# A graph network on one core: relation tables made bare inside the edge MLP's loop, their gate and bias applied in the relation pass

## The chip, the cores and the metric

The kernel runs on one core of a Trainium2 chip. The metric is the device time of one execution in microseconds (us). Before the change the median of three runs is 4499.05 us (4494.59 to 4503.68).

## The reference

Four graph layers work on 6250 nodes of 128 features and 106250 edges (50000 random pairs in both directions and a loop for every node, sorted by destination). After each, the result is added to the nodes and layer-normalised.

```python
x = _layernorm(x + gat_0(x, src, dst))
x = _layernorm(x + edge_mlp(x, src, dst, edge_attr_32))
x = _layernorm(x + relations(x, src, dst, edge_type_8))
x = _layernorm(x + gat_1(x, src, dst))

# edge_mlp, per edge, then per node
h   = gelu(_layernorm(concat(x[src], edge_attr) @ W1 + b1))
agg = segment_sum(h @ W2 + b2, dst)
out = gelu(_layernorm(concat(x, agg) @ Wu + bu)) + x

# relations: 8 relation types, one matrix, bias and gate each
msg  = (h @ W[rel])[src] + bias_term[rel]
gate = sigmoid(sum(msg * gate_weight[rel]) + gate_bias[rel])
out  = relu(segment_sum(msg * gate, dst) + h @ loop_weight)
```

The gate's argument is linear in the node's row, so it can be had from one product of the node with a matrix of 128 x 8 folded from W and the gate weights, plus a folded bias.

## The kernel before

The nodes are 49 tiles of 128, kept in SBUF. The edges are 104 groups (NG) of 1024, each group 8 tiles of 128 edges. A pass over the edges works through the groups in order: GpSimd (POOL) fetches the source rows of a group from a table in device memory with eight indirect DMAs (831 in a pass, since the last group is not full) into a ring of 8 groups (RING); a matrix of zeros and ones, made by VectorE (DVE) from the destinations, turns the sum over destinations into matmuls on TensorE (PE); DVE adds each group's sums (`p_sum`, PSUM) into the node accumulator `acc`. There are four such passes: attention (L723, gathers at L840), the edge MLP (`mlp_pass` L1464, gathers at L1593), relations (`rel_pass` L1192, gathers at L1254) and attention again.

The work on nodes is cut into 13 units of four tiles (the last two have three and two). Each engine's program is written out in order: step by step, an engine does its stage for group `step - lag`, and then the pieces of the units whose start `unit.at` plus the piece's lag is that step (`drive` L609, `weave` L619, where the order within a step is written). A unit starts when the groups that hold its edges have been summed, and at least six groups (APART) after the unit before; the last two start at steps 100 and 106. Engines meet at semaphores alone, and each stands still at a wait until it is met.

In a step of the MLP loop PE multiplies edge attributes (L1872), DVE adds them to the gathered rows (L1624), ScalarE (ACT) squares (L1789) and takes a root (L1791), DVE scales (L1630, L1632), ACT applies the gelu (L1799), and PE sums (L1889), into two alternating banks. DVE adds the sums (L1646) three steps after the gather. A unit's pieces follow: the node product, an inner normalisation, its gelu, the residual (L1722), the outer normalisation.

The relation tables, 49 tiles of 128 nodes x 8 relations x 128 features, are made after all sums of the MLP loop have been added (`sums_done`): PE turns the node tiles (L1938), ACT copies them out (L1843), PE makes the gate products (L1946) and the products with the relation matrices (L1954), both in PSUM banks that the loop used. DVE adds the gate bias (L1739), ACT takes the sigmoid (L1849), DVE adds the relation's bias to a whole tile while taking it out of PSUM (L1746) and multiplies half of it by the gate (L1750), ACT the other half (L1855), and SP stores the tile with one 512 KB transfer (L1574). The relation pass's first gather waits for all stores. In that pass a row of the table is a finished message of 512 bytes: it is gathered, and summed with the one-hot matrix (L1281, L1411, L1287).

Of the kernel before, what the change touches and what calls it, by code (L numbers as in the profile page):

```python
# [23 lines left out]
P = 128  # L24
# [9 lines left out]
RING = 8  # L34
HALF = 4
# [7 lines left out]
NORMED_AT = 14  # L43
ONE, AS = F, F + 1
TAB = AS + 2 * H
SUMS = AS + H
EPS = 1e-5
# [6 lines left out]
Unit = namedtuple("Unit", "u first tiles after at tab")  # L54
OfTable = namedtuple("OfTable", "lag")
# [12 lines left out]
def units_of(n, e, nt, ng):  # L68
# [8 lines left out]
    for u, m in enumerate(sizes):  # L77
        end = (first + m) * P
        after = ng - 1 if end >= n else min(ng - 1, -(-(end + SLACK) * e // (n * GE)) - 1)
        at = max(after, at + APART)  # L80
        units.append(Unit(u, first, m, after, at, 0))
        first += m
    start, end = ng + 2, at + NORMED_AT + 1
    spread = [start + (end - start) * unit.u // max(1, len(units) - 1) for unit in units]
    return tuple(unit._replace(tab=max(at, unit.at + NORMED_AT + 1)) for unit, at in zip(units, spread))

# [46 lines left out]
class Net:  # L133


    def __init__(self, nc, ctx, sh, ins, out):
# [23 lines left out]
        self.rel_b = sb("rel_b", [P, R, F])  # L160
# [14 lines left out]
        self.rel_table = dram("rel_table", (sh.NP * R, F))  # L175
# [414 lines left out]
def begins(unit, lag):  # L590

    return unit.tab + lag.lag if isinstance(lag, OfTable) else unit.at + lag
# [84 lines left out]
def landed(sh, n):  # L677


    return 16 * sum(len(given(sh, k)) for k in range(n % RING, n + 1, RING))  # L680

# [510 lines left out]
def rel_pass(net):  # L1192
# [3 lines left out]
    names = ["always", "weights_in", "onehot", "summed", "added", "index_in", "pool_passed", "sp_passed", "dve_passed", "act_passed", "pe_passed",  # L1196
             "x_turned", "xt_ready", "node_product", "variance", "rooted", "factors", "normed", "new_turned", "new_ready", "tab_product",
             "tab_done", "kept", "stored0", "stored1", "bound", "bound_all"]
    with phase(net, names, ["gathered"], RING) as s:
# [3 lines left out]
        rows = s.sb("rows", [P, RING, T, F])  # L1203
        hot = s.sb("hot", [P, HALF, T, P])
        lw = s.sb("lw", [P, F])
# [20 lines left out]
        def _(sp):  # L1226
            def load_slow(g):
                sp.dma_start(idx[:, :], net.rel_index[:, bass.ds(g, 1), :].rearrange("p g t -> p (g t)")).then_inc(s.index_in, 16)
                sp.dma_start(dsts[:, :], a["dst_cols"][bass.ds(g, 1), :, :].rearrange("g p t -> p (g t)")).then_inc(s.index_in, 16)
                sp.wait_ge(s.added, (g + 1) * sh.NT)  # L1230
                sp.sem_inc(s.sp_passed, 1)
# [5 lines left out]
            sp.dma_start(lw[:, :], a["L2_gnn_loop_weight"]).then_inc(s.weights_in, 16)  # L1237

# [11 lines left out]
        def _(pool):  # L1250
# [8 lines left out]
            def gather_slow(g):  # L1259
                pool.wait_ge(s.index_in, (g + 1) * 32)  # L1260
# [17 lines left out]
        def _(dve):  # L1278
# [3 lines left out]

            def add(n):
                first = window(dve, net, n)
                dve.wait_ge(s.summed, n + 1)
                part = net.acc[:, 0, bass.ds(first, P)]
                nc.vector.tensor_tensor(part, part, p_sum[n % 2][:, 0:P], ALU.add)  # L1287
                dve.drain().then_inc(s.added, 1)

            def residual(unit):  # L1290
# [4 lines left out]
                nc.vector.memset(net.acc[:, 0, columns(unit)], 0.0)  # L1295
# [24 lines left out]
            def slow_group(g):  # L1320
                dve.wait_ge(s.index_in, (g + 1) * 32)
                dve.wait_ge(s.gathered[0], (g + 1) * 16 * T)
                dve.sem_inc(s.dve_passed, 1)

            def slow_window(v, k):
# [6 lines left out]
                part = net.acc[:, 0, bass.ds(k * P, P)]  # L1332
                nc.vector.tensor_tensor(part, part, p_sum[0][:, 0:P], ALU.add)
                dve.drain().then_inc(s.added, 1)

            nc.vector.tensor_copy(p_iota[:, :], net.iota_row[:, :])
            dve.drain().then_inc(s.always, 1)
# [30 lines left out]
        def _(act):  # L1368
            def copy_x(unit):
# [27 lines left out]
            def fast():  # L1397
                drive(sh, [], pieces)

            def slow():  # L1400
                drive_units(sh, pieces)
# [3 lines left out]
        def _(pe):  # L1405
            def add_up(n):
                pe.wait_ge(s.onehot, n + 1)
                pe.wait_ge(s.gathered[n % RING], landed(sh, n))
                wait(pe, s.added, n - 1)
                for t in range(T):  # L1410
                    end = nc.tensor.matmul(p_sum[n % 2][:, 0:P], rows[:, n % RING, t, :], hot[:, n % HALF, t, :], start=(t == 0), stop=(t == T - 1))  # L1411
                end.then_inc(s.summed, 1)
# [7 lines left out]
            def multiply(unit, fast):  # L1420
# [23 lines left out]
            def slow_window(v, k):  # L1444
                pe.wait_ge(s.onehot, v + 1)
                for t in range(T):
                    end = nc.tensor.matmul(p_sum[0][:, 0:P], rows[:, 0, t, :], hot[:, 0, t, :], start=(t == 0), stop=(t == T - 1))
                end.then_inc(s.summed, 1)
# [4 lines left out]
            def fast():  # L1453
                drive(sh, [(add_up, 0)], pieces(True))
# [5 lines left out]
            pe.wait_ge(s.weights_in, 16)  # L1460
# [3 lines left out]
def mlp_pass(net):  # L1464
# [4 lines left out]
             "x_turned", "xt_ready", "node_product", "variance", "rooted", "factors", "inner_normed", "node_scaled", "activated", "normed", "tab_turned", "tab_copied", "gate_product", "gate_logits", "gate_ready", "tab_product", "tab_read", "dve_scaled", "act_scaled",  # L1469
             "index_in", "pool_passed", "sp_passed", "dve_passed", "act_passed", "pe_passed"]  # L1470
    with phase(net, names, ["gathered"], RING, ["operands_in", "hot_in"], HALF, ["stored"], TABS) as s:
# [3 lines left out]
        rows = s.sb("rows", [P, RING, T, HID])  # L1475
# [581 lines left out]
```

## Time and profile before

| what | time |
|---|---|
| median of three runs | 4499.05 us |
| the profiled execution, its span | 5314.6 us |
| PE busy | 3112.7 us (59%) |
| DVE busy | 2515.0 us (47%) |
| ACT busy | 1308.4 us (25%) |
| POOL busy | 3165.2 us (60%) |

The profile is one execution of the program, and its span, the only time that it gives for itself, is 18% above the median. Busy times are of compute instructions and of POOL's gathers; the shares are averages over stages that differ. A row of a timeline gives start, duration, engine, line, what is written from what, and in brackets how long the engine had been idle and what released it ("issue" where it waited for nothing the profile shows, "remote" for a queue that it doesn't know).

### The profile page before, as it was taken

The numbers are of one execution on the slowest core, as the hardware profiler recorded it, in microseconds if no ns is written. First come the engines' busy times: TensorE is split into PE (matmuls) and PEld (weight loads), VectorE is DVE, ScalarE is ACT, GpSimd is POOL, SyncE is SP. The second block draws the span as 40 slices with busy tenths as digits, with TensorE's granted clock in tenths as the row PEclk, the third lists the DMA queues.
The fourth block names the chain that finished last, engine by engine and source line by source line (L and its number), as shares of the span: only waits on it lengthen the run. The fifth ranks groups of instructions, "written<-read, shape, count | busy, mean of one in ns | idle before, by whom it ended". The sixth has DMA issues, their size and how long they took to land. (4 is left out here: it accounts for less than half of the span.)

```text
span 5314.6 us, 52198 instructions
## 1 busy us (share of the span) xinstructions
PE 3112.7 (59%) x15416; PEld 2793.1 (53%) x15416; DVE 2515.0 (47%) x5316; ACT 1308.4 (25%) x3470; POOL 3165.2 (60%) x3335
## 2 busy tenths in 40 slices
PE   2666666666377787777871323333332666666666
PEld 2665666566366676666731223323231666666665
DVE  2344444445377878777870111112121454554555
ACT  0010010011267777777760000000000011111111
POOL 5666666663566666666206666666654666666662
PEclk6556556666689888988895566665665565555656
DMA  5444444443444444444241111111112333333331
GB/s 140 128 144 139 151 142 140 151 140 110 138 134 145 147 144 144 143 144 148 81 189 47 48 49 49 50 49 47 52 43 67 97 95 97 99 95 97 98 96 52
DMA packets 284107, 567.22 MB, mean 107 GB/s; under 512 B 108648, under 2 KB 157034, under 8 KB 283802
## 3 DMA queue, kind: packets, MB, share of 16 engines
q0 software_dynamic: 119664, 280.17, 20.3%
q1 hardware_dynamic: 157082, 278.92, 15.4%
q10 hardware_dynamic: 7056, 4.56, 0.3%
q8 instruction: 131, 2.15, 0.2%
q14 instruction: 174, 1.43, 0.1%
HBM read 465.83 MB, written 97.56 MB: 106 GB/s over the span
## 5 line engine op out<-in xcount | busy, mean ns | idle before, releaser
L840 POOL DMA_INDIRECT rows<-gat_table,src_i x1662 | 1568.6, 944 | 861.4 <-issue 464.9
L1593 POOL DMA_INDIRECT rows<-mlp_table,src_i x831 | 789.5, 950 | 527.0 <-issue 303.8
L1254 POOL DMA_INDIRECT rows<-rel_table,rel_i x831 | 783.9, 943 | 494.8 <-issue 343.4
L1129 PE MATMUL p_sum<-rows,hot 128*128 128x133 f32 x3328 | 781.6, 425 | 14.2 <-DVE rows L906 12.5
L1121 PEld LDWEIGHTS p_adc<-adw,hot_t 128*128 128x128 f32 x3328 | 688.1, 314 | 178.0 <-DVE hot_t L880 127.5
L1121 PE MATMUL p_adc<-adw,hot_t 128*128 128x8 f32 x3328 | 678.0, 342 | 147.7 <-DVE hot_t L880 108.4
L1129 PEld LDWEIGHTS p_sum<-rows,hot 128*128 128x128 f32 x3328 | 735.9, 326 | 17.2 <-DVE rows L906 15.6
L1411 PE MATMUL p_sum<-hot,rows 128*128 128x128 f32 x1664 | 324.5, 363 | 715.9 <-DVE hot L1281 365.9
L1411 PEld LDWEIGHTS p_sum<-hot,rows 128*128 128x128 f32 x1664 | 298.6, 272 | 744.3 <-DVE hot L1281 381.2
L1061 ACT COPY sums<-p_sum 128x133 f32<-128x133 f32 x208 | 56.4, 271 | 2211.6 <-DMA rel_index<-rel_i 1902.6
L1889 PE MATMUL p_sum<-hot,rows 128*128 128x128 f32 x3328 | 476.0, 310 | 201.8 <-ACT rows L1799 107.7
L1889 PEld LDWEIGHTS p_sum<-hot,rows 128*128 128x128 f32 x3328 | 461.3, 224 | 236.5 <-ACT rows L1799 123.5
L1136 PE MATMUL p_turn<-ident,sums 128*128 128x128 f32 x208 | 90.7, 436 | 781.1 <-ACT sums L1061 724.7
L906 DVE TENSOR_TENSOR rows<-rows,p_weight 128x1024 f32<-128x1024 f32 x208 | 253.7, 1220 | 610.5 <-ACT p_weight L1056 448.2
L1872 PE MATMUL p_pre<-w1e,eat 128*128 128x256 f32 x1664 | 436.8, 415 | 105.3 <-issue 104.4
L1136 PEld LDWEIGHTS p_turn<-ident,sums 128*128 128x128 f32 x208 | 35.5, 171 | 834.5 <-ACT sums L1061 772.8
L1287 DVE TENSOR_TENSOR acc_t<-acc_t,p_sum 128x128 f32 x104 | 29.8, 286 | 864.3 <-remote 775.9
L1872 PEld LDWEIGHTS p_pre<-w1e,eat 128*128 128x128 f32 x1664 | 337.3, 209 | 172.5 <-issue 123.3
L1789 ACT ACTIVATE junk<-rows 128x256 f32<-128x256 f32 x832 | 335.6, 404 | 294.5 <-DVE rows L1624 179.0
L1624 DVE TENSOR_TENSOR rows<-rows,p_pre 128x1024 f32<-128x1024 f32 x208 | 247.6, 1218 | 281.1 <-PE p_pre L1872 112.2
L1630 DVE SCALAR_TENSOR_TENSOR rows<-rows,stats,p_affine 128x256 f32<-128x256 f32 x832 | 335.1, 475 | 8.3
L886 DVE TENSOR_TENSOR z<-rows,p_adc 128x32 f32<-128x32 f32 x208 | 39.0, 188 | 561.1 <-remote 312.0
(239 smaller groups left out, 3693.9 us busy)
## 6 DMA issues: line engine op xcount, KB each, us to landing
drow<-in_dst_rows SPq DMA_DIRECT2D x208, 512.0 KB
hot_table<-hot SPq DMA_DIRECT2D x104, 512.0 KB
hot<-hot_table SPq DMA_DIRECT2D x104, 512.0 KB
rows<-gat_table,src_i POOLq DMA_INDIRECT x1662
rel_table<-rows SPq DMA_DIRECT2D x49, 512.0 KB, 2.6
eat<-in_edge_t SPq DMA_DIRECT2D x104, 128.0 KB
rows<-mlp_table,src_i POOLq DMA_INDIRECT x831
rows<-rel_table,rel_i POOLq DMA_INDIRECT x831
```

The source lines that it names most:

```text
L840: pool.indirect_dma_start(out=rows[:, n % RING, t, :], out_offset=None, in_=net.gat_table[:, :], in_offset=bass.IndirectOffsetOnAxis(ap=ne ...
L906: nc.vector.tensor_tensor(hr, hr, wt, ALU.mult).then_inc(s.messages, 1)
L1121: end = nc.tensor.matmul(p_adc[k][:, t, 0:2 * H], hot_t[:, k, t * P:(t + 1) * P], adw[:, half, :], start=True, stop=True)
L1129: end = nc.tensor.matmul(p_sum[:, 0:SUMS], hot[:, n % HALF, t, :], rows[:, n % RING, t, 0:SUMS], start=(t == 0), stop=(t == T - 1))
L1254: pool.indirect_dma_start(out=rows[:, n % RING, t, :], out_offset=None, in_=net.rel_table[:, :], in_offset=bass.IndirectOffsetOnAxis(ap=ne ...
L1411: end = nc.tensor.matmul(p_sum[n % 2][:, 0:P], rows[:, n % RING, t, :], hot[:, n % HALF, t, :], start=(t == 0), stop=(t == T - 1))
L1593: pool.indirect_dma_start(out=rows[:, n % RING, t, :], out_offset=None, in_=net.mlp_table[:, :], in_offset=bass.IndirectOffsetOnAxis(ap=ne ...
L1624: nc.vector.tensor_tensor(rows[:, slot, tt, :], rows[:, slot, tt, :], p_pre[half][:, :, :], ALU.add).then_inc(s.pre, 1)
L1630: nc.vector.scalar_tensor_tensor(rows[:, slot, t, :], rows[:, slot, t, :], stats[:, slot, 1, t:t + 1], p_affine[:, 0, :], ALU.mult, ALU.mult)
L1789: nc.scalar.activation(junk[:, t % (T // 2), :], rows[:, slot, t, :], ACT.Square, accum_out=stats[:, slot, 0, t:t + 1])
L1872: end = nc.tensor.matmul(p_pre[half][:, j, :], eat[:, ring, half, :], w1e[:, j, :], start=True, stop=True)
L1889: end = nc.tensor.matmul(p_sum[k][:, b, :], rows[:, n % RING, t, b * F:(b + 1) * F], hot[:, half, t, :], start=(t == 0), stop=(t == T - 1))
```

## The change

The relation table holds the bare product of node and relation matrix, and in a column of its own the gate's argument: rows of 129 values (REL) in place of 128. It is made inside the MLP loop, unit by unit, as soon as the unit's nodes are normalised: a turn at lag 15, the gate product at lag 16, and from lag 16 on a tile per step in two halves of four relations. PE makes a half in one PSUM bank `pt`, which holds the gate product too, in the columns of its first use; ACT alone copies it to one of four slots of `stage`, with the gate's arguments beside it; SP stores it (98 stores of 264 KB instead of 49 of 512 KB). To make room, the loop's sums have one bank instead of two (PE's sums of a group wait for DVE's add of the group before), the ring is 7 groups deep, and the relations' bias, 128 x 1024 in SBUF before, is no longer kept. DVE's order in a step begins with the add.

In the relation pass ACT takes the sigmoid of the gathered column (128 x 8 a group), DVE makes a matrix of edge by relation type, multiplies it and the gathered rows by the gate, and PE sums both with the one-hot matrix: the rows as before and, in eight matmuls more, the gates by type. DVE adds these to `acc` too, and the bias enters at the unit's product, as one more matmul of the summed gates with the 8 x 128 bias matrix. PE's sums come one step later than before, DVE's add two.

```diff
+MLP_RING = 7
+TURN_AT = NORMED_AT + 1
+GATE_AT = TURN_AT + 1
+REL = F + 1
 # relation pass
+            def kinds(half, given):
+                nc.vector.tensor_tensor(kind[:, half, :, :], tiled(given, T, R), over_tiles(net.iota_row[:, 0:R], T, R), ALU.is_equal)
+                dve.drain()
+            def weighted(slot, half, k):
+                nc.vector.tensor_tensor(kind[:, half, :, :], kind[:, half, :, :], tiled(gate[:, k, :], T, R), ALU.mult)
+                nc.vector.tensor_tensor(rows[:, slot, :, 0:F], rows[:, slot, :, 0:F], tiled(gate[:, k, :], T, F), ALU.mult)
+                return dve.drain()
+            def weigh(n):
+                kinds(n % HALF, types[:, n, :])
+                dve.wait_ge(s.gated, n + 1)
+                weighted(n % RING, n % HALF, n % 2).then_inc(s.weighed, 1)
...
+                nc.vector.tensor_tensor(gates, gates, p_sum[n % 2][0:R, P:2 * P], ALU.add)
...
-                drive(sh, [(one_hot, 0), (add, 1)], pieces)
+                drive(sh, [(one_hot, 0), (weigh, 1), (add, 2)], pieces)
...
+            def gates(n):
+                act.wait_ge(s.gathered[n % RING], landed(sh, n))
+                wait(act, s.weighed, n - 1)
+                nc.scalar.activation(gate[:, n % 2, :], rows[:, n % RING, :, F], ACT.Sigmoid).then_inc(s.gated, 1)
...
+                for t in range(T):
+                    nc.tensor.matmul(p_sum[k][0:R, P:2 * P], kind[:, half, t, :], hot[:, half, t, :], start=(t == 0), stop=(t == T - 1))
...
+                    nc.tensor.matmul(pu[:, t, :], net.acc[0:R, 1, cols], rb[:, :], start=False, stop=False)
 # MLP pass
-                    nc.vector.tensor_tensor(tab, p_tab[t % 2], net.rel_b[:, :, :], ALU.add).then_inc(s.tab_read, 1)
...
-                    nc.vector.tensor_tensor(tab[:, 0:by_dve, :], tab[:, 0:by_dve, :], tiled(gate[:, k, i, 0:by_dve], by_dve, F), ALU.mult).then_inc(s.dve_scaled, 1)
...
+            def copy_new(unit):
+                dve.wait_ge(s.new_turned, unit.u + 1)
+                nc.vector.tensor_copy(turned[:, 0:unit.tiles, :], pt[:, 0:unit.tiles, :]).then_inc(s.new_copied, 1)
...
+            def keep(unit, i, q):
+                h = part_of(unit, i, q)
                 act.wait_ge(s.gate_logits, unit.u + 1)
+                act.wait_ge(s.tab_product, h + 1)
+                wait(act, s.stored[h % TABS], 16 * (h // TABS))
+                nc.scalar.copy(staged(h)[:, :, F], logit[:, i, q * R // 2:(q + 1) * R // 2])
+                nc.scalar.copy(staged(h)[:, :, 0:F], pt[:, :, :]).then_inc(s.second_kept if q else s.first_kept, 1)
...
+            def fill(unit, i, q):
+                if q:
+                    pe.wait_ge(s.first_kept, unit.first + i + 1)
+                elif i:
+                    pe.wait_ge(s.second_kept, unit.first + i)
+                else:
+                    pe.wait_ge(s.gate_logits, unit.u + 1)
+                four = slice(q * R // 2, (q + 1) * R // 2)
+                nc.tensor.matmul(pt[:, :, :].rearrange("p r f -> p (r f)"), turned[:, i, :], net.rel_w[:, four, :].rearrange("p r f -> p (r f)"),
+                                 start=True, stop=True).then_inc(s.tab_product, 1)
...
-                wait(pe, s.added, n - 1)
+                wait(pe, s.added, n)
...
-                drive(sh, [(pre, 0), (add, 3), (scale, 1)], pieces(True))
+                weave(sh, [(add, 3, False), (pre, 0, False)] + [(fn, lag, True) for fn, lag in tables] + [(scale, 1, False)] + [(fn, lag, True) for fn, lag in weights + steps])
...
-                drive(sh, [(edges, 0), (add_up, 2)], pieces(True))
+                weave(sh, [(edges, 0, False)] + [(fn, lag, True) for fn, lag in turns + seconds] + [(add_up, 2, False)]
+                      + [(fn, lag, True) for fn, lag in pieces(True) + firsts])
```

## Rows read from the trace of the kernel before

**Rows 1.** Windows: the stages; busy us (x count), granted clock, DMA share, GB/s.
```profile
0.00:1430.00 1430.00, 859.75 (x4013) 792.66 (x4014) 623.58 (x1431) 129.90 (x460) 856.39 (x903) 0.61 0.47 138
1430.00:2600.00 1170.00, 908.78 (x5135) 801.41 (x5134) 910.73 (x1648) 850.22 (x2100) 729.02 (x767) 0.88 0.45 142
...
2900.00:4000.00 1100.00, 369.34 (x1958) 340.05 (x1959) 197.88 (x423) 43.67 (x95) 703.55 (x746) 0.61 0.19 48
4000.00:5315.00 1315.00, 805.08 (x3654) 751.71 (x3652) 631.38 (x1553) 158.91 (x490) 785.01 (x832) 0.59 0.33 90
...
```

**Rows 2.** Gather lines: ns min/median/max, first and last start; idle by releaser.
```profile
L840 POOL DMA_INDIRECT rows<-gat_table,src_i x1662: 938/944/1100, 51.1 to 5229.4; - x185
...
L1593 POOL DMA_INDIRECT rows<-mlp_table,src_i x831: 940/946/1324, 1339.3 to 2575.0; - x167
...
L1254 POOL DMA_INDIRECT rows<-rel_table,rel_i x831: 938/944/956, 2790.2 to 3967.9; - x167
...
  issue: 343.4, 799
...
```

**Rows 3.** Timeline of POOL in the MLP loop: start, us, instruction [idle before].
```profile
1530.83 0.95 POOL L1593 DMA_INDIRECT rows<-mlp_table,src_i  x1 [0.30 <-issue]
1532.09 0.95 POOL L1593 DMA_INDIRECT rows<-mlp_table,src_i  x1 [0.31 <-issue]
1535.14 0.95 POOL L1593 DMA_INDIRECT rows<-mlp_table,src_i  x1 [2.10 <-remote]
...
```

**Rows 4.** Windows summed over eleven stretches of the loop, and its scale line.
```profile
sum 1080.00, PE 838.67 PEld 738.56 DVE 837.88 ACT 788.04 POOL 690.27; mean PE 76.24 PEld 67.14 DVE 76.17 ACT 71.64 POOL 62.75
...
L1632 DVE TENSOR_TENSOR rows<-rows,p_affine x104: 2286/2287/2289, 1419.2 to 2637.4; 128x2048 f32<-128x2048 f32 x104
...
```

**Rows 5.** Timeline, DVE then POOL: the stretch between the two passes.
```profile
2645.63 0.42 DVE L1646 TENSOR_TENSOR acc_t<-acc_t,p_sum 128x256 f32 x1 [0.90 <-PE p_sum L1889]
...
2653.26 1.22 DVE L1746 TENSOR_TENSOR rows<-p_pre,rel_b 128x1024 f32<-128x1024 f32 x1
...
2790.21 0.95 POOL L1254 DMA_INDIRECT rows<-rel_table,rel_i  x1 [100.11 <-issue]
...
```

**Rows 6.** Lines of that stretch: busy us, mean ns, idle before.
```profile
L1954 PE MATMUL p_pre<-rel_w,hot 128*128 128x512 f32 x196 | 98.1, 647 | 8.8 <-DVE rows L1746 8.8
...
L1746 DVE TENSOR_TENSOR rows<-p_pre,rel_b 128x1024 f32<-128x1024 f32 x49 | 59.7, 1219 | 10.4 <-PE p_pre L1954 10.4
...
L1750 DVE TENSOR_TENSOR rows<-rows,gate 128x512 f32<-128x512 f32 x49 | 33.9, 692 | 8.9 <-ACT gate L1849 4.7
...
L1946 PE MATMUL p_affine<-rel_gate,hot 128*128 128x8 f32 x98 | 12.6, 254 | 3.3 <-ACT hot L1843 3.3
L1938 PE MATMUL p_sum<-ident,x_nodes 128*128 128x128 f32 x49 | 8.0, 284 | 7.4 <-ACT hot L1843 7.4
...
L1843 ACT COPY hot<-p_sum 128x512 f32<-128x512 f32 x11 | 6.2, 567 | 6.0 <-PE p_sum L1938 5.1 <-issue 0.9
...
```

**Rows 7.** Timeline of DVE: a node update's moments.
```profile
2646.61 0.86 DVE L1699 SCALAR_TENSOR_TENSOR o<-w2u,degree,pu 128x128 f32<-128x128 f32 x3 [0.56 <-PE pu L1929]
...
2648.95 0.18 DVE L705 RECIPROCAL work<-work 128x3 f32<-128x3 f32 x1
...
```

**Rows 8.** The table store, L1574: issue to landing.
```profile
DMA to landing us min/median/max: 2.6/2.6/3.8
```

**Rows 9.** The page's costliest groups: the relation pass's sums.
```profile
L1411 PE MATMUL p_sum<-hot,rows 128*128 128x128 f32 x1664 | 324.5, 363 | 715.9 <-DVE hot L1281 365.9
...
```

**Rows 10.** Timeline, all engines, near the MLP loop's last gathers.
```profile
2561.95 2.29 DVE L1632 TENSOR_TENSOR rows<-rows,p_affine 128x2048 f32<-128x2048 f32 x1
2563.09 0.95 POOL L1593 DMA_INDIRECT rows<-mlp_table,src_i  x1 [0.30 <-issue]
2564.16 0.68 DVE L1722 SCALAR_TENSOR_TENSOR x_nodes<-x_nodes,o 128x512 f32<-128x512 f32 x1
...
2564.34 1.32 POOL L1593 DMA_INDIRECT rows<-mlp_table,src_i  x1 [0.30 <-issue]
...
```

More of the change, by code:

```diff
@@ L53 @@
 Shapes = namedtuple("Shapes", "N E NT NP NW NG NB NBATCH BN units")
-Unit = namedtuple("Unit", "u first tiles after at tab")
-OfTable = namedtuple("OfTable", "lag")
+Unit = namedtuple("Unit", "u first tiles after at")
 def shapes_of(n, e):
@@ L80, in units_of @@
         at = max(after, at + APART)
-        units.append(Unit(u, first, m, after, at, 0))
+        units.append(Unit(u, first, m, after, at))
         first += m
-    start, end = ng + 2, at + NORMED_AT + 1
-    spread = [start + (end - start) * unit.u // max(1, len(units) - 1) for unit in units]
-    return tuple(unit._replace(tab=max(at, unit.at + NORMED_AT + 1)) for unit, at in zip(units, spread))
+    return tuple(units)
 def least_bases(sh):
@@ L590, in begins @@
 def begins(unit, lag):
-    return unit.tab + lag.lag if isinstance(lag, OfTable) else unit.at + lag
+    return unit.at + lag
 def run_units(sh, step, pieces):
@@ L674, in given, with landed @@
     return range(min(T, -(-(sh.E - n * GE) // P)))
-def landed(sh, n):
-    return 16 * sum(len(given(sh, k)) for k in range(n % RING, n + 1, RING))
+def landed(sh, n, ring=RING):
+    return 16 * sum(len(given(sh, k)) for k in range(n % ring, n + 1, ring))
 def tiles_of(unit):
@@ L1405, in _, with sums @@
         def _(pe):
+            def sums(k, slot, half):
+                for t in range(T):
+                    nc.tensor.matmul(p_sum[k][0:R, P:2 * P], kind[:, half, t, :], hot[:, half, t, :], start=(t == 0), stop=(t == T - 1))
+                for t in range(T):
+                    end = nc.tensor.matmul(p_sum[k][:, 0:P], rows[:, slot, t, 0:F], hot[:, half, t, :], start=(t == 0), stop=(t == T - 1))
+                return end
             def add_up(n):
                 pe.wait_ge(s.onehot, n + 1)
-                pe.wait_ge(s.gathered[n % RING], landed(sh, n))
+                pe.wait_ge(s.weighed, n + 1)
                 wait(pe, s.added, n - 1)
-                for t in range(T):
-                    end = nc.tensor.matmul(p_sum[n % 2][:, 0:P], rows[:, n % RING, t, :], hot[:, n % HALF, t, :], start=(t == 0), stop=(t == T - 1))
-                end.then_inc(s.summed, 1)
+                sums(n % 2, n % RING, n % HALF).then_inc(s.summed, 1)
             def turn_x(unit):
@@ L1445, in slow_window @@
                 pe.wait_ge(s.onehot, v + 1)
-                for t in range(T):
-                    end = nc.tensor.matmul(p_sum[0][:, 0:P], rows[:, 0, t, :], hot[:, 0, t, :], start=(t == 0), stop=(t == T - 1))
-                end.then_inc(s.summed, 1)
+                sums(0, 0, 0).then_inc(s.summed, 1)
             def pieces(fast):
@@ L1585, in _ @@
             for k in range(TABS):
-                wait(sp, s.stored[k], 16 * sum(unit.tiles for unit in sh.units[k::TABS]))
+                wait(sp, s.stored[k], 16 * len(range(k, 2 * sh.NT, TABS)))
         @s.block.gpsimd
@@ L1947, in fill_tab @@
                 end.then_inc(s.gate_product, 1)
-                pe.wait_ge(s.pre, 2 * sh.NG)
-                for i in range(unit.tiles):
-                    t = unit.first + i
-                    wait(pe, s.tab_read, t - 1)
-                    for q in range(2):
-                        four = slice(4 * q, 4 * q + 4)
-                        end = nc.tensor.matmul(p_tab[t % 2][:, four, :].rearrange("p r f -> p (r f)"), node_xt(unit)[:, i, :],
-                                               net.rel_w[:, four, :].rearrange("p r f -> p (r f)"), start=True, stop=True)
-                    end.then_inc(s.tab_product, 1)
+            def fill(unit, i, q):
[8 more added lines that the diff above has]
+                                 start=True, stop=True).then_inc(s.tab_product, 1)
```

203 lines of the change are left out of this document (95 added, 108 removed).

## The prediction

> **What bounds the kernel now.** I read the totals by stage first. In each of the four stages that gather (two attention passes, the edge MLP, the relation pass) POOL has the most evenly filled row, and the stages differ in what works beside it [rows 1]. Then the gather lines: 831 gathers a pass, 0.94 us each, and POOL idle before them mostly for "issue", that is, for nothing the profile shows [rows 2]. Where POOL runs freely, gathers start 1.25 us apart: 0.94 plus 0.30 [rows 3]. So a group of eight costs 10.0 us and a pass of 831 cannot be under 1039 us. In the profile the MLP's gathers take 1235.7 us (1339.3 to 2575.0) and the relation pass's 1177.7 [rows 2].
>
> The span is 5314.6 us and the timed median 4499: the profiled execution is 815.6 us longer. The two passes just named stand 336 us over POOL's pace; if the attention passes stand as far over, that is some 670 of the 815. I therefore read the timed kernel as four passes at or near POOL's pace, and the stretches between them as about what the profile shows. The terms below are sums of durations of single instructions and of such a stretch; they are made against the span, and I carry the same number of microseconds over to the median.
>
> The MLP loop is the one with little room. Its step in the profile is (2637.4 − 1419.2)/103 = 11.83 us [rows 4], of which POOL works 10.0 and then waits about 2.1 before the next group [rows 3]. Over 1080 us of the loop PE is busy 838.7, DVE 837.9 and ACT 788.0 [rows 4]: per step 9.2, 9.2 and 8.6 us. In the relation pass (2900 to 4000, 93 groups of gathers) PE is busy 4.0 us a group, DVE 2.1, ACT 0.5 [rows 1].
>
> Between these two passes lies a stretch without gathers: the last sum is added at 2645.63 and the relation pass's first gather starts at 2790.21 [rows 5]. 49 table tiles are made there, each held by DVE: bias 1.22 us plus half the gate products 0.69, 1.91 us to the next tile [rows 5, 6]; 49 × 1.91 = 94 us.
>
> **The change part by part.**
>
> *The table stretch.* From 2646.05 (end of that add) to 2790.21 are 144.2 us. DVE's adds and products of bias and gate (59.7 + 33.9 [rows 6]) go, and ACT's share of the products with them. What must stay is the chain of the last unit, since its rows exist only once all sums do: moments of a node update twice, 2.5 us each (2646.61 to 2649.13 [rows 7]), and between and behind them eleven small steps of ACT and DVE (two roots with a table load, factors, two normalisations, affine, gelu with its load, residual), estimated at 1 us each by the 0.6 to 1.2 us of the copies and adds in [rows 6] and a hand-over: 16 us; turn, copy, gate product and logits 2; then four half-tiles, each a product (98.1/98 = 1.0 us) and a copy (0.57 [rows 6], a small one of 0.2 by estimate, and two hand-overs of 0.15), 1.9 each, 7.7; the last store's landing 2.6 [rows 8]. With the unit's first turning and product (2 to 3) that is 31 us. The pieces run at one lag per step, 18 steps past the unit's start, behind the previous unit's on every in-order engine; that may double it. I take 49, nearest to the middle, with ends at 31 and 65: −95 us, ends −79 and −113. The store goes past SP's loads of hot rows and edge data, which by then have ended.
>
> *The MLP loop.* Added per pass: on ACT 98 half-tile copies of 0.57 and 98 logit copies of about 0.2, 75 us or 0.7 a step; on PE products 98.1, gates 12.6, turns 8.0 [rows 6], 119 us or 1.14 a step; on DVE 13 copies and 13 adds, about 10 us. SP gets 98 stores, of which each waits for ACT's copy and stands ahead of later loads of hot rows; the loads have HALF groups of lead, so a wait under a step costs nothing. Busy time per step becomes PE 10.3, DVE 9.3, ACT 9.3. PE is then above POOL's 10.0, but these are the profile's busy times, at a granted clock of 0.88, a mix of the 1.2 and 2.4 GHz levels [rows 1], and with matmul ends that are modelled. The single sum bank makes PE's next sums wait for DVE's add, which now comes first in DVE's step: behind that wait on PE stand the unit's products and the next edge products, for which DVE's next pre-activation waits. The half-tile's product waits for ACT's copy of the half before. A ring of 7 instead of 8 leaves 70 us of gathers ahead, enough where POOL is the bound. Bounds: 0, when the timed step keeps to POOL's 10.0, and 1.14 us a step × 104 = 119 (PE's added work wholly exposed). I take 0.3 a step, +30, nearer to the lower end because in the 11.83-us step every engine's row leaves at least 2 us before the change and 1.5 after it.
>
> *The relation pass.* DVE gains per group a comparison and a product of 128x64, an add of 8x128 and the row product of 128x1024, 1.22 us by the nearest row of that size [rows 6]. DVE goes from 2.1 to about 4 us of 10; PE doubles its sum instructions, 324.5/104 = 3.1 us a group more [rows 9], to 7.1 of 10, with one more product per tile of a unit; ACT's sigmoid is 0.2. All of that lies beside POOL. What doesn't is a disturbance between DVE and POOL. At 2564.16 DVE started an add whose inputs both lie in SBUF (node rows and their update, 0.68 us); the gather that began at 2564.34 took 1.32 instead of 0.95. The gather at 2563.09 ran beside the 2.29-us add whose second input is in PSUM, and took 0.95 [rows 10]. The new row product has both inputs in SBUF, in a pass that POOL bounds. The Trainium skill ("SBUF — State Buffer", Who interferes with whom) says that a DVE instruction with two SBUF inputs and a GpSimd instruction that reads SBUF exclude each other; the trace agrees with 1.32 against 0.95, and if it did not hold for gathers of this pass the sum would be 42 us lower. The delay seen ends where DVE's add ends (2564.84, 0.38 us after the gather would have gone on), so a group can lose from 0 (the product falls between two gathers' reads) to 1.22 us (it starts just ahead of one): 0 to 127 us for 104 groups. The product follows the group's landing and ACT's sigmoid, so its place against the gathers is about the same in every group; I take 0.4, which is the 0.37 of the row, +42.
>
> *The relation pass's end.* After the last gather come in addition the sigmoid 0.2, DVE's products 1.6, and PE's second set of sums 3.1 to 5.8 (16 × 0.363 [rows 9]): +8, ends 3 and 10. The start gains one load of a small bias matrix and one DVE instruction on types, both ahead of the first gather's landing. Rows of 516 instead of 512 bytes change nothing I can price: the attention table's rows, 548 bytes, are gathered in the same 0.94 us [rows 2].
>
> Sum: −95 + 30 + 42 + 8 = −15: a span of 5300 and a median of 4484.
>
> **The rivals.**
>
> *All hidden.* The loop has room for the tables, and the row product falls between gathers: −95 + 8 = −87, 4412. For it: POOL's 2.1-us waits in the loop, and DVE, busy 198 of 1100 us in the relation pass [rows 1], can take the products as rows land. Against: PE's 10.3 us a step.
>
> *The port.* The row product blocks the gather for most of its length, 0.9 us a group: 94 instead of 42, net +37, 4536. For it: one gather starts every 1.25 us and the product takes 1.22, so some gather is nearly always in the way. Against: each is delayed only from its read to the product's end, on average half the length.
>
> *PE bounds the MLP loop* (the other side). Each step waits for edge products, a half-tile's two products, sums, and a unit's pieces in one order on PE, and a sum that waits for the gelu and for the add leaves a hole that later products can't fill. At 1.14 us a step exposed, +119 instead of +30: net +74, 4573. It decides above 0.43 us a step, the point at which the gain (95 − 42 − 8 = 45) is spent. For it: 10.3 against 10.0. Against: the busy times are those of an execution 18% longer than the timed one.
>
> **How the numbers follow.** Forecast 0.40, all hidden 0.22, the port 0.17, PE 0.21. The forecast's own range is 4455 to 4510. A measurement of this kernel can tell about 0.2%, 9 us, from no change. Of the forecast's 0.40 I give 0.29 to faster, 0.09 to within 9 us, 0.02 to slower; all hidden is faster; of the port 0.04 is within and 0.13 slower; of PE 0.02 faster (a half-exposed step with a shorter tail), 0.02 within, 0.17 slower. Faster 0.53, within 0.15, slower 0.32. For 8 in 10 the range goes from 4405, just under all hidden, to 4560, which leaves out the upper part of the PE case.
>
> **What would show it.** From the last add of the MLP pass to the first relation gather: some 50 us instead of 144. Relation gathers that take 1.2 to 1.4 us, one or so in eight, each beside the row product; if all stay at 0.94, the +42 is wrong. The MLP step: 11.83 or little more shows the loop holding; over 12.5, with PE's products waiting for ACT's copies or POOL's first gather of a group waiting longer for sums, shows the PE rival. The forecast is wrong altogether if the tail stays above 100 us, because the empty steps are long, or if the relation pass becomes bound by DVE or PE.

## The result and the profile after

The change made the kernel 0.44% slower: 4520.34 us (4516.4 to 4522.79, 4 runs) against 4500.74, ratio 1.0044 with a 95% interval of 1.003 to 1.0058. Forecast was 4484, faster. The time lies inside the range that was given, on the other side of no change.

The profiled execution of the kernel before had been 18% longer than its timed ones; the changed kernel's is not (4517.6 us). For a fair comparison the kernel before was profiled once more, unchanged: its span there is 4497.4 us, and wherever "before" has numbers below, they are from that execution. It answers [rows 2] and [rows 5] so: gather lines with duration min/median/max in ns and first and last start in us, then, from the timeline, the last add of the MLP pass and the first relation gather.

> The kernel before, unchanged, profiled once more, because its first profiled execution was 18% longer than its timed ones (5314.6 against 4499.05 us) while the one of the changed kernel is not (4517.6). Theory 1 (the loop and the port took the gain): in an undisturbed execution the relation pass's gathers span 1035 to 1042 us against 1066 after the change, the edge MLP's about 1040 against 1060, and the stretch between them about 190 against 147, so the stretch's gain is some 40 us, not 95. Rival (the stretch gave nothing): the stretch between last MLP gather and first relation gather is at 150 us or below already, and the whole 20 us come from the relation pass. A span near 4499.

```profile
L1593 POOL DMA_INDIRECT rows<-mlp_table,src_i x831: 942/947/1453, 1125.0 to 2167.1; - x167
...
L1254 POOL DMA_INDIRECT rows<-rel_table,rel_i x831: 940/945/958, 2342.6 to 3379.7; - x167
```

```profile
2198.23 0.42 DVE L1646 TENSOR_TENSOR acc_t<-acc_t,p_sum 128x256 f32 x1 [0.89 <-PE p_sum L1889]
...
2342.57 0.95 POOL L1254 DMA_INDIRECT rows<-rel_table,rel_i  x1 [99.88 <-issue]
```

Theory 1 is the nearer of the two. The gathers span 1042.1 and 1037.1 us, as it has them. The stretch from the last MLP gather to the first relation gather is 175.5 us against 147.1 after the change: a gain of 28 us, not 40, and not nothing.

The same lines of the changed kernel (L1593 has become L1636, L1254 has become L1261, L1646 has become L1689):

```profile
L1636 POOL DMA_INDIRECT rows<-mlp_table,src_i x831: 940/946/1457, 1125.4 to 2185.9; - x167
...
L1261 POOL DMA_INDIRECT rows<-rel_table,rel_i x831: 940/944/1336, 2333.0 to 3399.4; - x167
```

```profile
2252.94 0.42 DVE L1689 TENSOR_TENSOR acc_t<-acc_t,p_sum 128x256 f32 x1 [0.83 <-PE p_sum L1911]
...
2333.00 0.95 POOL L1261 DMA_INDIRECT rows<-rel_table,rel_i  x1 [52.31 <-issue]
```

From these rows the whole difference of the spans, 20.2 us, can be laid out. All times in us:

| stretch | before | after | difference |
|---|---|---|---|
| MLP gathers, first to last start | 1042.1 | 1060.5 | +18.4 |
| last gather to the start of the last add | 31.1 | 67.1 | +36.0 |
| last add to the first relation gather | 144.3 | 80.1 | −64.2 |
| relation gathers, first to last start | 1037.1 | 1066.4 | +29.3 |
| relation pass's end, up to the next gather | 42.0 | 42.8 | +0.8 |
| all the rest | | | −0.1 |

The reader is to see three things. The stretch that the change aims at did shrink, by 64 us. The MLP loop, first gather to last add, grew by 54, and two thirds of that don't stand in the gathers' span at all: the sums fall behind the gathers, and POOL's ring hides this until the gathers end. And the relation pass, whose gathers before went at POOL's own pace, is 29 us longer.

How much room each engine had in the loop is seen in the undisturbed execution. Windows of 800 us of the loop, before and after; columns are length, then busy time (and count) of PE, PE's weight loads, DVE, ACT and POOL, then granted clock, share of DMA and GB/s:

```profile
1300.00:2100.00 800.00, 666.34 (x4147) 602.47 (x4147) 734.22 (x1356) 684.60 (x1704) 605.63 (x638) 0.94 0.55 170
```

```profile
1300.00:2100.00 800.00, 699.51 (x4152) 614.76 (x4153) 702.46 (x1309) 690.62 (x1748) 595.85 (x628) 0.93 0.60 186
```

Before, 638 gathers are 80 groups: DVE is busy 9.2 us of each 10.0, ACT 8.6, PE 8.3. DVE had the least room, 0.8 us a step. After, DVE adds the sums of 76 groups in this window instead of 80. Per group it is busy about as long (9.24 us against 9.18), but it stands idle for 97.5 us in place of 65.8.

### The profile page after: what moved, and what is told of

The parts are those of the page before. It is cut to its first block and busy times, and to the rows that moved or that the text cites. A ratio compares the mean times of both kernels' runs of the same rounds, so it can differ in the third digit from the quotient of the medians.

```text
span 4517.6 us, 56537 instructions
## 1 busy us (share of the span) xinstructions
PE 3249.7 (72%) x17178; PEld 2793.7 (62%) x17178; DVE 2603.7 (58%) x5648; ACT 1339.2 (30%) x3564; POOL 3197.3 (71%) x3335
## 5 line engine op out<-in xcount | busy, mean ns | idle before, releaser
L1261 POOL DMA_INDIRECT rows<-rel_table,rel_i x831 | 814.4, 980 | 305.3 <-issue 305.3
L1121 PE MATMUL p_adc<-adw,hot_t 128*128 128x8 f32 x3328 | 643.8, 331 | 507.4 <-DVE hot_t L880 507.1
L1636 POOL DMA_INDIRECT rows<-mlp_table,src_i x831 | 789.3, 950 | 308.5 <-issue 285.6
L1121 PEld LDWEIGHTS p_adc<-adw,hot_t 128*128 128x128 f32 x3328 | 627.6, 290 | 574.6 <-DVE hot_t L880 573.7
L1451 PE MATMUL p_sum<-hot,kind 128*8 128x128 f32 x1664 | 330.5, 382 | 438.7 <-issue 415.6
L1911 PE MATMUL p_sum<-hot,rows 128*128 128x128 f32 x3328 | 453.4, 302 | 135.0 <-DVEq L1690 84.2
L1911 PEld LDWEIGHTS p_sum<-hot,rows 128*128 128x128 f32 x3328 | 439.5, 216 | 177.3 <-ACT rows L1832 123.1
L1451 PEld LDWEIGHTS p_sum<-hot,kind 128*8 128x8 f32 x1664 | 194.6, 120 | 552.0 <-issue 457.7
L1894 PE MATMUL p_pre<-w1e,eat 128*128 128x256 f32 x1664 | 385.2, 385 | 23.2 <-DVEq L1804 18.7
L1296 DVE TENSOR_TENSOR kind<-kind,gate 128x64 f32<-128x64 f32 x104 | 23.4, 225 | 573.8 <-ACT gate L1403 573.8
L880 DVE TENSOR_TENSOR hot_t<-drow,p_adc 128x1024 f32<-128x1024 int32 x208 | 253.9, 1221 | 16.0 <-issue 0.4
```

The source lines that it names most:

```text
L880: nc.vector.tensor_tensor(hot_t[:, k, :], drow[:, half, :], p_base.broadcast_to([P, GE]), ALU.is_equal).then_inc(s.turned_onehot, 1)
L1121: end = nc.tensor.matmul(p_adc[k][:, t, 0:2 * H], hot_t[:, k, t * P:(t + 1) * P], adw[:, half, :], start=True, stop=True)
L1261: pool.indirect_dma_start(out=rows[:, n % RING, t, :], out_offset=None, in_=net.rel_table[:, :], in_offset=bass.IndirectOffsetOnAxis(ap=ne ...
L1451: nc.tensor.matmul(p_sum[k][0:R, P:2 * P], kind[:, half, t, :], hot[:, half, t, :], start=(t == 0), stop=(t == T - 1))
L1636: pool.indirect_dma_start(out=rows[:, n % MLP_RING, t, :], out_offset=None, in_=net.mlp_table[:, :], in_offset=bass.IndirectOffsetOnAxis(a ...
L1894: end = nc.tensor.matmul(p_pre[half][:, j, :], eat[:, ring, half, :], w1e[:, j, :], start=True, stop=True)
```

## The experiments

**The port, tested in the relation pass.** The gates go to PSUM, so that no DVE product of the pass has both inputs in SBUF; ScalarE's sigmoid waits one group longer.

```diff
-        gate = s.sb("gate", [P, 2, T])
+        gate = s.ps("gate", [P, 2, T])
-    ... over_tiles(net.iota_row[:, 0:R], T, R), ALU.is_equal)
+    ... over_tiles(p_iota[:, 0:R], T, R), ALU.is_equal)
-                wait(act, s.weighed, n - 1)
+                wait(act, s.weighed, n)
```

> The changed kernel with the gates of a group in a PSUM bank instead of SBUF, and the comparison of types against the iota in PSUM: every DVE product and comparison of the relation pass has an operand in PSUM, ScalarE's sigmoid waits for the products of the group before. Nothing else is changed. Theory 1 (DVE's two SBUF inputs hold up the gathers): the relation gathers' mean falls from 980 to 945 ns, their span from 1066 to about 1038 us, and the time from 4520 to 4493 (4488 to 4498), which is faster than before the change. Rival (the relation pass is long because TensorE's doubled sums or the longer chain hold the ring): gathers stay near 980 ns or wait between groups, and the time stays within 5 us of 4520.

Measured: 4492.85 us, ratio to before 0.9975 (0.9965 to 0.9985), so the change with this edit is faster than before. The relation gathers span 1037.1 us again, and their mean is 944.8 ns against 980.0. Two places of the timelines show it; first the changed kernel, a product of rows and gate (L1297) and the gathers around it:

```profile
2601.30 0.95 POOL L1261 DMA_INDIRECT rows<-rel_table,rel_i  x1 [0.30 <-issue]
...
2601.74 1.22 DVE L1297 TENSOR_TENSOR rows<-rows,gate 128x1024 f32<-128x1024 f32 x1
...
2602.55 1.23 POOL L1261 DMA_INDIRECT rows<-rel_table,rel_i  x1 [0.30 <-issue]
...
2604.08 0.94 POOL L1261 DMA_INDIRECT rows<-rel_table,rel_i  x1 [0.30 <-issue]
```

and the same product with its gate in PSUM:

```profile
2605.11 0.94 POOL L1261 DMA_INDIRECT rows<-rel_table,rel_i  x1 [0.30 <-issue]
...
2605.48 1.21 DVE L1297 TENSOR_TENSOR rows<-rows,gate 128x1024 f32<-128x1024 f32 x1
...
2606.36 0.94 POOL L1261 DMA_INDIRECT rows<-rel_table,rel_i  x1 [0.30 <-issue]
```

In both a gather begins some 0.3 to 0.4 us before the product's end (2602.96 and 2606.69). With the gate in SBUF it takes 1.23 us, with the gate in PSUM 0.94. So it is not the product's place in time that changed, but its operand. In the changed kernel 103 of the 831 gathers take over 1.1 us, about one for each of the 104 groups, and each of the 103 ends 0.81 to 0.82 us behind the end of the product that it lies beside. With the gate in PSUM none takes over 0.96. The doubled sums on TensorE and the longer chain cost nothing here. The rule of the Trainium skill ("SBUF — State Buffer", Who interferes with whom), that a DVE instruction with two SBUF inputs contends with a GpSimd instruction that reads SBUF, is borne out by both halves of this pair.

**The tables' work in the loop.** TensorE's half-tile products and ScalarE's copies are left out, the semaphores passed on, and the stage buffer, set to zero once, is stored as before. The relation tables then hold nothing of use.

```diff
-                nc.tensor.matmul(pt..., turned[:, i, :], net.rel_w[:, four, :]..., ...).then_inc(s.tab_product, 1)
+                pe.sem_inc(s.tab_product, 1)
-                nc.scalar.copy(staged(h)[:, :, F], logit[:, i, q * R // 2:(q + 1) * R // 2])
-                nc.scalar.copy(staged(h)[:, :, 0:F], pt[:, :, :]).then_inc(...)
+                act.sem_inc(s.second_kept if q else s.first_kept, 1)
```

> The changed kernel without the half-tile products on TensorE and without ScalarE's copies: the two engines only pass the semaphores, the stores still move the stage buffer (set to zero once), so the tables hold nothing of use. Turns, gate products and logits stay. Theory 1 (the tables' work in the loop is not hidden, TensorE is the bound there): the edge MLP's gathers span 1040 instead of 1060 us and the sums' backlog after the last gather shrinks from 67 us to under 45; with some 15 us less behind the last sum, the time falls by 45 to 70 us to about 4460. Rival (the loop would be as long without them, bound by DVE's steps; only the chain behind the last sum is long): the MLP's gathers and backlog change by under 8 us and the time falls by 10 to 20 us.

Measured: 4472.51 us, ratio to before 0.993 (0.9914 to 0.9945). The loop from first gather to last add falls from 1127.6 to 1109.9 us, the stretch behind it from 80.1 to 43.1. So the halves cost 17.7 us inside the loop and 37 behind it; the backlog after the last gather is still 61.8 us. Neither theory had that: the loop stays 37 us longer than before with no half made in it, so TensorE's products are not its main cost, and behind the last sum the halves cost more than twice what I had put down. The time fell by 48 us, which theory 1 had (45 to 70), but that is luck: the MLP's gathers span 1048.1 us instead of its 1040, and the backlog is 61.8 instead of under 45.

**The add's place in DVE's step.** Waits of DVE in the loop (1300 to 2100: us in total, times, longest) of the kernel before, then of the changed one:

```profile
DVE rows L1624 <- PE p_pre L1872: 19.5, 28, 3.6
DVE rows L1624 <- issue: 6.9, 37, 0.2
DVE rows L1624 <- DMA rows<-mlp_table,src_i: 5.3, 10, 0.9
```

```profile
DVE acc_t L1689 <- issue: 40.1, 45, 1.2
DVE rows L1667 <- PE p_pre L1894: 22.9, 38, 1.4
DVE rows L1667 <- issue: 11.1, 57, 0.5
```

The first row of the changed kernel has no counterpart: 40 us ahead of the add, in 45 of the 76 steps, waiting for nothing the profile shows. The add's address is read into a register by the instruction ahead of it. In the timeline of the changed kernel a step that ends in small unit pieces shows the idle time (behind a 2.29-us scaling there is none), and in the kernel before, where the pre-activation stands ahead, the add follows at once:

```profile
1606.13 0.69 DVE L1759 TENSOR_TENSOR o<-o,vec 128x512 f32<-128x512 f32 x1
1607.91 0.42 DVE L1689 TENSOR_TENSOR acc_t<-acc_t,p_sum 128x256 f32 x1 [1.08 <-issue]
1608.52 2.35 DVE L1667 TENSOR_TENSOR rows<-rows,p_pre 128x1024 f32<-128x1024 f32 x2 [0.19 <-issue]
```

```profile
1610.97 2.35 DVE L1624 TENSOR_TENSOR rows<-rows,p_pre 128x1024 f32<-128x1024 f32 x2 [0.19 <-issue]
1613.24 0.41 DVE L1646 TENSOR_TENSOR acc_t<-acc_t,p_sum 128x256 f32 x1
```

Three kernels test this. In the kernel before, the order alone:

```diff
-                drive(sh, [(pre, 0), (add, 3), (scale, 1)], pieces(True))
+                drive(sh, [(add, 3), (pre, 0), (scale, 1)], pieces(True))
```

> The kernel before with one edit: DVE's add of three groups before stands ahead of the pre-activation in its step, as in the changed kernel; two sum banks, no tables in the loop. Theory W: the loop from first gather to last add grows from 1073 to about 1115 us, the time from 4500 to 4540 (4530 to 4550). Rival S: with two sum banks the place of the add is free, the time stays within 5 us of 4500.

Measured: 4535.55 us against 4505.17, ratio 1.0071 (1.0054 to 1.0088). The gathers' span stays (1041.4 us), the backlog goes from 31.1 to 64.9, and the wait ahead of the add appears:

```profile
DVE acc_t L1646 <- issue: 38.7, 45, 1.2
DVE rows L1624 <- PE p_pre L1872: 20.1, 33, 2.1
DVE rows L1624 <- issue: 11.2, 58, 0.5
```

The loop grows from 1073.2 to 1106.3 us. These 33 us are the order's, with two sum banks and no table in the loop. In the changed kernel, the register read alone, moved behind the scaling:

```diff
+            def look(n):
+                firsts[n] = window(dve, net, n)
             def add(n):
-                first = window(dve, net, n)
...
-        weave(sh, [(add, 3, False), (pre, 0, False)] + ... + [(scale, 1, False)] + ...)
+        weave(sh, [(add, 3, False), (pre, 0, False)] + ... + [(scale, 1, False), (look, 2, False)] + ...)
```

> The changed kernel; in the edge MLP's loop DVE reads the register with the place of the next add right behind the scaling of the step before, not at the add. Nothing else moves. Theory W (with the add first in DVE's step, the register read stands between DVE's pieces and its add with nothing left running, some 0.8 us a step): DVE's idle time before the add falls from 43 us (1300 to 2160) to under 10, the loop from the first gather to the last add from 1127.6 to about 1085 us, the time from 4520 to 4478 (4470 to 4488). Rival S (the single sum bank and the tables' products on TensorE set the step): the idle time turns up before the edge sums instead, the loop stays above 1115 us and the time above 4508.

Measured: 4509.0 us, ratio to before 1.0008 (0.9998 to 1.0018), where the changed kernel had 1.0044; its span is 19 us shorter, its loop 1107.9 us, where the changed kernel had 1127.6:

```profile
DVE rows L1667 <- PE p_pre L1898: 37.3, 47, 2.5
DVE rows L1667 <- issue: 10.1, 52, 0.5
DVE acc_t L1693 <- issue: 9.9, 45, 0.2
```

The wait ahead of the add falls from 40.1 to 9.9 us, as theory W has it, but 14 us come back as waits for the edge products, which rival S had named: the gain is 19 us of span (0.36 points, 16 us, by the ratios), not 42. Neither theory holds whole: the loop is shorter than rival S has it, the time longer than theory W's. In the changed kernel, the old order with the single bank:

```diff
-                weave(sh, [(add, 3, False), (pre, 0, False)] + ...
+                weave(sh, [(pre, 0, False), (add, 3, False)] + ...
```

> The changed kernel with DVE's old order in the edge MLP's loop: the pre-activation first, then the add of three groups before; the sum bank stays single. Theory W: DVE's idle time before the add goes, the loop comes to 1085 to 1100 us, the time to 4480 to 4495, a little above the early register read, since TensorE's sums wait longer for the add. Rival S: TensorE's wait for DVE's add (76 us from 1300 to 2160) grows, edge products come later, the loop gets longer than 1127 us and the time is above 4520.

Measured: 4589.2 us, ratio 1.0189 (1.0172 to 1.0206). Theory W fails here and rival S holds: DVE doesn't wait ahead of the add any more, but TensorE's sums wait for the add, and DVE for the edge products queued behind them on TensorE. The second fence is TensorE's wait in the same stretch, of the same kernel; the third is that wait in the changed kernel:

```profile
DVE rows L1667 <- PE p_pre L1894: 94.0, 78, 5.1
```

```profile
PE p_sum L1911 <- DVEq L1690: 138.1, 71, 4.7
```

```profile
PE p_sum L1911 <- DVEq L1690: 72.7, 24, 5.0
```

So the two belong together. With a single sum bank the old order makes the loop 63 us longer (1191.0 against 1127.6), and the new order costs 33 us even with two banks. That the change puts the add first because of the single bank is my reading of it; tables in the loop with two sum banks and the old order were not run.

Four of the kernels lay out the loop's growth in one chain, each with the loop from first gather to last add in us:

| kernel | loop | step |
|---|---|---|
| before | 1073.2 | |
| before, add first in DVE's step | 1106.3 | +33.0 |
| changed kernel without the halves | 1109.9 | +3.6 |
| changed kernel | 1127.6 | +17.7 |

The third row has the single bank, the ring of 7, the turns, the gate products and the stores; once the add goes first, all of these together cost 3.6 us.

**The halves behind the last sum.** The last units' halves, in the changed kernel (PE makes a half, ACT copies the gate's arguments and then the half):

```profile
2316.77 2.07 PE L1976 MATMUL pt<-rel_w,turned 128*128 128x512 f32 x2 [0.27 <-DVE logit L1784]
2318.93 0.20 ACT L1876 COPY stage<-logit 128x4 f32<-128x4 f32 x1 [4.70 <-issue]
2319.03 0.58 ACT L1877 COPY stage<-pt 128x512 f32<-128x512 f32 x1
2319.66 2.07 PE L1976 MATMUL pt<-rel_w,turned 128*128 128x512 f32 x2 [0.81 <-ACT stage L1877]
```

A half takes 2.89 us from start to start, 2.07 for the product and 0.81 in which TensorE waits for ScalarE's copy. The copies' line has 20 of them behind the last add:

```profile
L1877 ACT COPY stage<-pt 128x512 f32<-128x512 f32 x20 | 11.6, 578 | 0.0
```

The first two halves behind the last add are shorter, 1.94 us from start to start: their products take 1.12 us, at a granted clock of 0.99 (2253 to 2258). From 2258 to the end of the stretch the granted clock is 0.50, the lower of its two levels (1.2 GHz), and the other 18 halves go at 2.07 and 2.89. Together the 20 halves are some 56 of the stretch's 80 us.

```profile
2253.53 1.12 PE L1976 MATMUL pt<-rel_w,turned 128*128 128x512 f32 x2
...
2255.47 1.12 PE L1976 MATMUL pt<-rel_w,turned 128*128 128x512 f32 x2 [0.81 <-ACT stage L1877]
```

For the last three units the second halves were put into a bank that the edge products no longer need:

```diff
+        def bank(unit, q):
+            return p_pre[0][:, 0:2, :]... if q and late(unit) else pt[:, :, :]...
...
+                if q and late(unit):
+                    pe.wait_ge(s.pre, 2 * sh.NG)
+                    wait(pe, s.second_kept, unit.first + i)
...
-                nc.tensor.matmul(pt..., turned[:, i, :], ...
+                nc.tensor.matmul(bank(unit, q), turned[:, i, :], ...
```

> The changed kernel; for the last three units (nine tiles, all of whose halves are made after the last group's pre-activation) the second halves go to a PSUM bank that the edge products used, so TensorE makes a half while ScalarE copies the other. Theory T (behind the last sum the halves' round trips through one bank, 2.9 us each of which the product is 2.1, set the time): the stretch from the last add to the first relation gather falls from 80.1 to 65 to 70 us, the time from 4520 to about 4507. Rival (the last unit's node chain sets it, halves of earlier units lie beside it): the stretch changes by under 4 us.

Measured: 4508.49 us, ratio to before 1.0006 (0.9996 to 1.0016); the stretch falls from 80.1 to 62.8 us, somewhat more than expected. Products now follow each other, for the three tiles of one unit and then the two of the last:

```profile
2289.66 2.08 PE L1987 MATMUL pt<-rel_w,turned 128*128 128x512 f32 x2 [0.28 <-DVE logit L1790]
...
2296.25 1.02 PE L1987 MATMUL pt<-rel_w,turned 128*128 128x512 f32 x2
...
2303.59 2.07 PE L1987 MATMUL pt<-rel_w,turned 128*128 128x512 f32 x2 [0.27 <-DVE logit L1790]
...
2305.45 1.91 PE L1987 MATMUL p_pre<-rel_w,turned 128*128 128x512 f32 x2
```

Two things changed at once here. TensorE no longer stands idle for 0.81 us behind each product, and the granted clock no longer stays low: it is 0.50 from 2285 to 2295 and 0.93 from 2295 to 2300, behind products that followed one another, and the product falls from 2.08 us to 1.02. So some of the 17 us can be the clock's; the two were not tested apart.

**Together.** The three edits in one kernel:

> The changed kernel with the three edits that each took time away: gates of the relation pass in PSUM, the early register read in the MLP loop, two banks for the last halves. Theory (three separate places: the port in the relation pass, DVE's register read in the loop, the halves' round trips behind the last sum): the gains add, 28 + 19 + 17 us of span, so 4517.6 becomes 4453 and the median some 4456 to 4462, about 1% under the kernel before. Rival (they share a cause, for example the clock granted to TensorE or DMA traffic): the sum falls short by more than 10 us, the median above 4470.

Measured: 4455.39 us, ratio 0.9888 (0.9871 to 0.9904): 1.1% under the kernel before. The relation gathers span 1036.0 us, the stretch behind the last add is 62.9, the loop 1104.9. Against the changed kernel's 1.0044 that is 1.56 points of the time before; the single gains, 0.69, 0.36 and 0.38, make 1.43. So they add, and the rival of a shared cause falls.

One more place: beside GpSimd's clearing of the sums, a DVE instruction on 128x3 elements took 4.48 us instead of 0.17 in the changed kernel.

```profile
2276.24 4.48 DVE L703 TENSOR_SCALAR work<-work 128x3 f32<-128x3 f32 x1
```

```diff
-            pool.wait_ge(s.node_product, len(sh.units))
+            pool.wait_ge(s.normed, len(sh.units))
```

> The same with GpSimd's clearing of the sums moved from behind the last node product to behind the last normalisation, so that it doesn't lie beside DVE's moments (in the changed kernel one small DVE instruction took 4.48 us beside it instead of 0.17). Theory (it stands in the last units' chain): the stretch from the last add to the first relation gather shrinks by 3 to 5 us, the time by the same. Rival (TensorE's halves set the stretch): it stays within 1 us of all_three.

Measured: 4459.83 us, ratio 0.9896 (0.988 to 0.9913); against all_three's 0.9888 no gain, and by the medians 4 us more, which the rival didn't have either. The theory fails as a whole, and half of it was right: counted from the last add, the last unit's logits start 3.2 us earlier (47.1 against 50.3 us), but the first relation gather comes 4.3 us later (67.2 against 62.9 us). The clearing now ends at 2288.03, 2 us behind ScalarE's last copy, and from its end to the first gather are 11.56 us in which POOL waits for nothing the profile shows. POOL is not alone: SP's first load of the relation pass starts at 2298.26, in all_three at 2290.79. And such a gap is there without the edit too: at the end of the relation pass, where POOL's reduction is its last instruction, 9.44 us lie before the next pass's first gather in the kernel before and 9.51 in the changed one. The edit put the clearing where such a gap shows; what it consists of stays open.

## Why the prediction was wrong

*The bound.* That POOL's pace bounds the four passes held: gathers at 1037 to 1039 us a pass before, in all passes but the MLP (1042). That the MLP loop has little room held too, but the engine was wrong. I put TensorE first, by 10.3 us a step; in the undisturbed execution DVE was nearest to the bound, 9.2 of 10.0. The prediction took room from the 11.83-us step of its profile. Divided by POOL's 10.0 us, which the same rows gave, [rows 4] put PE and DVE at 92% alike, so they could not tell the two apart; in the undisturbed execution PE needs 8.3 us a step at a granted clock of 0.94, where [rows 1] have 0.88.

*The MLP loop, +30: it was +54. This is one of the two steps that failed.* I priced the tables' work on TensorE, and named the add's new place without a price of its own: "DVE's add, which now comes first in DVE's step". By the chain of kernels above the order is 33 of the 54 us and the halves 17.7. The bound of 119 had room for it, the value didn't.

*The table stretch, −95: it was −64. This is the other step that failed, and the larger: 31 us, outside its own bounds of −79 and −113.* The sum has the chain of the last unit, with its four halves at 1.9 us each, and the units ahead of it only as "that may double it". But halves start 16 steps after their units do, so those of the last three units, and two of the unit ahead, come behind the last add: 20 halves. The price of 1.9 had the turns of TensorE and ScalarE at one bank in it, and it held for the two halves at the high clock (1.94). It was too low for the other 18, which took 2.89: the product, 1.0 us in [rows 6], takes 2.07 at a granted clock of 0.50. Without halves the stretch is 43.1 us, where the 49 without its four halves leave 41, so what I had put down for everything else was not far off.

*The port, +42: it was +29.3.* Mechanism and place were right; the size was 0.28 us a group instead of 0.40. In all 103 gathers that were held the end followed the product's end at the same distance (0.81 to 0.82 us), so the size is set by how long before the product's end a gather begins. The bounds were 0 and 1.22 a group.

*The relation pass's end, +8: it was +0.8.* That the second set of sums and the products lie beside other work there is likely, not shown.

*The sum.* The stretch came out 31 us worse than forecast and the loop 24, the port 13 better and the pass's end 7: from −15 to +20. With the stretch alone as forecast the change would have been some 11 us faster, with the loop alone as forecast 4, which is too little to tell from none. That the port and the end took back 20 of the 55 us is luck.

The rivals: "all hidden" was wrong in both halves. "The port" had 94 us where 29 came, further off than the forecast. "PE bounds the MLP loop" came in part: the loop did grow, and at 54/104 = 0.52 us a step it is above the 0.43 at which that rival decides. But 33 of the 54 us are DVE's order, and the halves, TensorE's products and ScalarE's copies together, are 18.

## What to carry to other kernels

Before a change moves work into a loop, divide every engine's busy time per step by the pace of the unit that bounds the loop, not by the step that a disturbed profile shows; the engine with least room is the one whose order must not change unpriced. A new order is a part of the change with a price of its own: here it cost the loop 33 us, the tables' work 18. Where work is spread over units that lag, count what is still to come, of all units, when the loop ends: 20 halves here, not 4; and price it at the clock that is granted there. And in a pass bound by GpSimd's gathers, look for DVE products with both inputs in SBUF: one operand moved to PSUM gave 28 us back.

## What the runs showed of the hardware

DVE's add with its register read ahead of it: in the changed kernel (1300 to 2100) no idle time stood before the 31 adds that followed a 2.29-us instruction, and 0.83 to 1.19 us before the 45 that followed a unit piece of 0.69 us or less; in the kernel before, none before the 80 adds, which all followed a 1.22-us product. By moving the read alone, 40.1 us of idle time became 9.9. A gather's delay depends on the operands of DVE's product: beside products of 1.22 us it took 1.23 us with both inputs in SBUF and 0.94 with one in PSUM, and all 103 gathers that were held ended 0.81 to 0.82 us behind the product's end. A DVE instruction on 128x3 elements beside GpSimd's memset took 4.48 us and ended with the memset (both at 2280.7); with the memset moved away (all_four), none of that line behind the last add took over 0.17. TensorE's products at one bank, each followed by 0.81 us of idle time, went at a granted clock of 0.50 and took 2.07 us in each of the last 18 halves; in two banks, one behind another, they came to 1.02 us, with 0.93 granted from 2295 to 2300.
